# A one-core decoder layer: the first 1024 cross keys and values are made in the prologue, and the penalty rows are loaded ahead of the chunk's stores

## What is computed

```python
x = layernorm(x + self_attention(x))          # one key head and one value head shared by 16 query heads, no mask
x = layernorm(x + cross_attention(x, ctx))    # 6404 context keys, mask 1024 x 6404 (int32), 16 heads
x = layernorm(x + top1_experts(x))            # 8 experts, the best one times its softmax weight
```

## Time and profile before

| what | us |
|---|---|
| median of 3 runs | 467.17 (465.81 to 469.11) |
| profiled execution, its own time | 469.97 |
| its span in the profile | 467.7 |
| TensorE / VectorE / ScalarE / GpSimd busy | 440.9 / 396.7 / 358.4 / 245.1 |
| mean granted TensorE clock | 0.974 of full |

### The profile page before, as it was taken

The page is one execution under the profiler, slowest core; times in us unless marked ns, Lnnn a source line. Parts: engine busy times, 40 slices in busy tenths (PEclk is TensorE's granted clock), DMA queues, the critical chain, the costliest instruction groups (busy, mean ns, idle before and its releaser), DMA issues.

```text
span 467.7 us, 10803 instructions
## 1 busy us (share of the span) xinstructions
PE 440.9 (94%) x3885; PEld 176.7 (38%) x3887; DVE 396.7 (85%) x522; ACT 358.4 (77%) x704; POOL 245.1 (52%) x381
## 2 busy tenths in 40 slices
PE   8999999999899999799999999999999999999983
PEld 2433333333334443233343334333443443333441
DVE  4989999999699689689998999999999999941455
ACT  6328889688677877588968988889868788878723
POOL 4726879976799604122447644444447254320453
PEclk9889999999899999989999999999999999999978
DMA  5849968679680073211232346322212122110000
GB/s 129 322 115 315 283 218 297 264 263 332 228 329 13 3 135 80 65 45 46 84 90 69 101 93 111 92 60 58 88 51 70 39 81 69 47 29 26 5 22 25
DMA packets 24595, 56.07 MB, mean 120 GB/s; under 512 B 6442, under 2 KB 15928, under 8 KB 22492
## 3 DMA queue, kind: packets, MB, share of 16 engines
q0 software_dynamic: 7536, 37.91, 24.6%
q1 hardware_dynamic: 16424, 17.24, 14.1%
q10 hardware_dynamic: 580, 0.20, 0.2%
HBM read 45.60 MB, written 9.18 MB: 117 GB/s over the span
## 4 chain that ended last, share of the span: by engine, by line
PE 76%; DVE 10%; DMA 5%; issue 4%; ACT 2%; POOL 2%; POOLq 0%; DVEq 0%; ACTq 0%
PE O L1503 29%; PE ST L1739 15%; PE ST L1530 9%; PE RT L1732 7%; DVE mxs L935 6%; DMA Qs<-mxr 5%; PE RT L1518 4%; PE RT L1625 2%; PE ST L1632 2%; PE RT L1429 1%; PE O L1481 1%; ACT prob L1302 1%; PE RT L1587 1%; PE RT L1595 1%; DVE mxc L952 1%
## 5 line engine op out<-in xcount | busy, mean ns | idle before, releaser
L1302 ACT ACTIVATE prob<-ST 128x512 f32<-128x512 f32 x512 | 279.5, 599 | 59.0 <-PE ST L1530 29.3
L935 DVE TENSOR_REDUCE mxs<-RT 128x2 f32<-128x1024 f32 x128 | 153.0, 1222 | 14.6 <-PE RT L1518 13.5
L952 DVE TENSOR_REDUCE mxc<-RT 128x2 f32<-128x1024 f32 x128 | 152.8, 1221 | 5.8 <-PE RT L1732 5.4
L1739 PE MATMUL ST<-Qs,Kc 64*128 64x512 f32 x320 | 117.4, 450 | 0.0
L1732 PE MATMUL RT<-Kr,Qs 64*128 64x512 f32 (+1 forms) x384 | 114.4, 400 | 2.1 <-issue 2.1
L1503 PE MATMUL O<-prob,vst 128*9 128x256 f32 x1280 | 99.1, 381 | 1.7 <-ACT prob L1291 0.5
L1530 PE MATMUL ST<-Qs,Kself 64*128 64x512 f32 x256 | 96.7, 449 | 4.0 <-DMA Qs<-mxr 3.8
L1518 PE MATMUL RT<-Kself,Qs 64*128 64x512 f32 x256 | 89.3, 465 | 2.2 <-DVE Kself L912 0.9
L681 POOL DMA_DIRECT2D Kr<-kd x96 | 47.8, 502 | 75.9 <-PE RT L1732 60.8
L1503 PE MATMUL O<-prob,Vs 128*9 128x256 f32 x1024 | 81.0, 388 | 1.2 <-ACT osb L1246 0.3
L1739 PEld LDWEIGHTS ST<-Qs,Kc 64*128 64x128 f32 x320 | 50.5, 184 | 65.8 <-issue 38.7
(11 more groups left out here) (219 smaller groups left out, 327.4 us busy)
## 6 DMA issues: line engine op xcount, KB each, us to landing
big<-in_mask POOLq DMA_DIRECT2D x16, 1664.0 KB, 7.3
Kc<-kd POOLq DMA_DIRECT2D x64, 80.0 KB, 2.2
Kr<-kd POOLq DMA_DIRECT2D x64, 64.0 KB, 2.1
od_s<-osb SPq DMA_DIRECT2D x16, 128.0 KB, 2.5
kd<-Vx SPq DMA_DIRECT2D x4, 512.0 KB, 6.9
Qs<-qd_x SPq DMA_DIRECT2D x8, 256.0 KB
od_x<-osb SPq DMA_DIRECT2D x14, 128.0 KB, 1.7
Qs<-qd_s SPq DMA_DIRECT2D x12, 128.0 KB, 5.9
```

The lines of the kernel that those rows point to most:

```text
L935: freed(v.tensor_reduce(mxs[:, h % 2, c2, :].rearrange("p (f t) -> p f t", f=2)[:, :, q], bank[:, :].rearrange("p (f k) -> p f k", f=2), A ...
L952: return v.tensor_reduce(o[:, :, u % 4], src, AX.X, ALU.max)
L1302: freed(nc.scalar.activation(prob[:, s % SLOTS, f * HALF:(f + 1) * HALF], bank[:, :], ACT.Exp))
L1739: mm = mmul(o[:, :], Kc[STACK[f], b * P:(b + 1) * P], Qs[STACK[f], j, :], start=True, stop=not gen, skip_group_check=True)
```

## The change

* The loads of `wk_x`, `wv_x`, `bk_x` and the 1024 context rows `ctxn` (512 KB) move to the head of SyncE's queue, behind those of the self attention's small operands and ahead of `bo` and `x`.
* Beside rows 8 and 9 TensorE makes the keys (`first_keys`, one 512-column half each, into `ST[0]` and `ST[1]`), beside rows 11 and 13 the values (`first_values`, into `O` and `ST[0]`); row 10 keeps its `warm_up`, rows 12, 14 and 15 have nothing beside them.
* ScalarE evicts each half of the keys twice (rounded into `khi`, full into `kz`) and each half of the values once into a staging place `v_first`. GpSimd subtracts `khi` from `kz` behind its mask piece 0, and copies `v_first` into `Vx` at m = 13, ahead of the ones.
* The jobs at s = 42, 90 and 92 are gone with VectorE's and ScalarE's evictions there. The first self column waits for the new evictions.
* SyncE's turn h = 6 waits for GpSimd's subtraction, and the penalty rows are loaded in turn h = 13, ahead of the chunk's stores.

```diff
@@ RT_JOBS, ST_JOBS
-RT_JOBS = {42: ("k",), 76: ("s0 spread",), ...
+RT_JOBS = {76: ("s0 spread",), ...
-ST_JOBS = {66: ("bias",), 86: ("s0 turn",), 88: ("s0 q",), 90: ("v0",), 92: ("v1",), KV: ("vm",),
+ST_JOBS = {66: ("bias",), 86: ("s0 turn",), 88: ("s0 q",), KV: ("vm",),
+        v_first = vroom[:, 6 * HALF:8 * HALF]
@@ SyncE
             load(bv_s[:, :], row("bv_s").to_broadcast([P, DH]), "in_r")
+            for n_, b_ in (("wk_x", wk_x), ("wv_x", wv_x)):
+                load(b_[:, :], t[n_], "ctx_in")
+            load(bk_x[:, :], column("bk_x"), "ctx_in")
+            load(ctxn[:, :], t["ctxT"][:, KPAD - KS:KPAD], "ctx_in")
             load(bo["s"][:, :], row("bo_s").to_broadcast([P, D]), "in_bo")
...
-                if h == 4:
-                    load(ctxn[:, :], t["ctxT"][:, KPAD - KS:KPAD], "ctx_in")
                 if h in (6, 7, 8):
                     if h == 6:
-                        sp.wait_ge(S("rt_free"), number(RT_AT, "k"))
+                        sp.wait_ge(S("x_k_low"), 1)
...
                         load(pd[:, k * KC:(k + 1) * KC], penr[...], "pen_out")
-                if h == 14:
-                    more_keys()
                     sp.wait_ge(S("pen_out"), 16 * 5)
                     sp.wait_ge(S("k_clean"), 2)
                     for k_ in (Kr, Kc):
                         load(k_[PENROWS...], pd.to_broadcast([2, KUSE]), "pen_in")
+                if h == 14:
+                    more_keys()
@@ GpSimd
+                if m == 0:
+                    pool.wait_ge(S("x_k_full"), 2)
+                    g_.tensor_tensor(kz, kz, khi.bitcast(F32), ALU.subtract).then_inc(S("x_k_low"), 1)
                 if m in MAX_BETWEEN:
                     split_max(MAX_BETWEEN[m])
...
                 if m == 13:
                     pool.wait_ge(S("q_out"), 64)
+                    pool.wait_ge(S("x_v_copied"), 2)
+                    g_.tensor_copy(Vx[:, 0:SBLK, :, 0:DH], v_first.rearrange("p (b h d) -> p b h d", h=HEADS, d=DH)) \
+                        .then_inc(S("vx_first"), 1)
+                    pool.wait_ge(S("vx_first"), 1)
                     pool.wait_ge(S("kd_out"), 64)
@@ ScalarE
+            def first_keys(c):
+                w = slice(c * 512, c * 512 + 512)
+                act.wait_ge(S("x_k_ready"), c + 1)
+                act.wait_ge(S("ctx_in"), 64)
+                act.wait_ge(S("s_k_stack"), 2)
+                nc.scalar.activation(khi[:, w], ST[c][:, :], ACT.Identity, bias=bk_x[:, 0:1])
+                nc.scalar.activation(kz[:, w], ST[c][:, :], ACT.Identity, bias=bk_x[:, 0:1]).then_inc(S("x_k_full"), 1)
+            def first_values(k, bank):
+                act.wait_ge(S("x_v_ready"), k + 1)
+                act.wait_ge(S("q0_stack"), 2)
+                nc.scalar.copy(v_first[:, k * 512:(k + 1) * 512], bank[:, :]).then_inc(S("x_v_copied"), 1)
...
+            first_keys(0)
+            first_keys(1)
             max_copy(0, 2)
+            first_values(0, O)
+            first_values(1, ST[0])
@@ TensorE
                 if c == 0:
-                    pe.wait_ge(S("q_high"), 2)
-                    pe.wait_ge(S("q_full"), 2)
+                    pe.wait_ge(S("x_k_full"), 2)
+                    pe.wait_ge(S("x_v_copied"), 2)
...
+            def first_keys(c):
+                if c == 0:
+                    pe.wait_ge(S("ctx_in"), 64)
+                pe.wait_ge(S("q_high"), c + 1)
+                pe.wait_ge(S("q_full"), c + 1)
+                keys_into(ST[c], ctxn[:, c * 512:(c + 1) * 512], 512).then_inc(S("x_k_ready"), 1)
+            def first_values(k):
+                if k:
+                    pe.wait_ge(S("x_k_full"), 1)
+                values_into((O, ST[0])[k], ctxn, 4 * k, 4 * k + 4).then_inc(S("x_v_ready"), 1)
...
-                else:
+                elif r in (8, 9):
+                    first_keys(r - 8)
+                elif r in (11, 13):
+                    first_values((r - 11) // 2)
+                elif r == 10:
                     warm_up(O, 2)
```

More of the change, by code:

```diff
@@ L71, in place @@
     return (s - SELF) // NBLK, (s - SELF) % NBLK
-RT_JOBS = {42: ("k",), 76: ("s0 spread",), 79: ("s0 y",), 94: ("count",), 99: ("flags",), KV - 1: ("km",),
+RT_JOBS = {76: ("s0 spread",), 79: ("s0 y",), 94: ("count",), 99: ("flags",), KV - 1: ("km",),
            X(1, 3): ("s1 spread",), X(1, 5): ("s1 y",), X(9, 3): ("x0 spread",), X(9, 5): ("x0 y",),
@@ L261, in decoder_layer @@
             "mask_in0 mask_in1 mask_used mask_added mask_counts flags steered pen_made pen_out pen_in "
-            "ctx_in kd_out kd_more k_clean vx_ones kr0 kr1 kr2 kc0 kc1 vs0 vs1 mx_folded x_bias bias_tile dve_chain "
+            "ctx_in x_k_ready x_k_full x_k_low x_v_ready x_v_copied vx_first kd_out kd_more k_clean vx_ones kr0 kr1 kr2 kc0 kc1 vs0 vs1 mx_folded x_bias bias_tile dve_chain "
             "rt_ready rt_free st_ready st_free pv mx mx_part mx_split mx_turned mx_copied max_in0 max_in1 "
@@ L419, in _ @@
                 if h == 1:
-                    for n_, b_ in (("wq_x", wq_x), ("wk_x", wk_x), ("wv_x", wv_x)):
-                        load(b_[:, :], t[n_], "in_w")
+                    load(wq_x[:, :], t["wq_x"], "in_w")
                     for a, b_ in (("s", wo_s), ("x", wo_x)):
@@ L427, in _ @@
                     load(down[:, :], row("countdown").to_broadcast([P, NP]), "in_w")
-                    load(bk_x[:, :], column("bk_x"), "in_w")
                     load(bq["x"][:, :], column("bq_x"), "in_w")
@@ L633, in _ @@
                 if m == 7:
-                    pool.wait_ge(S("in_w"), 16 * 15)
+                    pool.wait_ge(S("in_w"), 16 * 12)
                     g_.tensor_copy(bv_wide[:, :], bv_x[:, :].to_broadcast([P, P])).then_inc(S("bias_tile"), 1)
@@ L799, in any_keys @@
                             cols_of(j + 1, None, pool.snap(n * (j + 1)))
-            pool.wait_ge(S("st_free"), number(ST_AT, "v1"))
+            pool.wait_ge(S("vx_ones"), 1)
             before = steps[0]
@@ L988, in cross_whole @@
                 whole_max(UNITS + U, mxc[:, U % 2, 0:2, :])
[L990 to L996, removed]
             def more_keys():
@@ L1135, in _ @@
                     dve.sem_inc(S("kd_more"), 1)
+                    dve.wait_ge(S("ctx_in"), 64)
                     more_keys()
@@ L1141, in _ @@
                 if s == 70:
-                    dve.wait_ge(S("in_w"), 16 * 15)
+                    dve.wait_ge(S("in_w"), 16 * 12)
                     mark(v.memset(downx[:, :], 0.0))
@@ L1153, in _ @@
                     residual("s", 0)
-                if s == 42:
-                    last_keys()
                 if s == 94:
@@ L1261, in x_queries @@
                 freed(nc.scalar.activation(xq_full[:, :], bank[:, :], ACT.Identity, bias=bq["x"][:, 0:1], scale=SCALE))
[L1263 to L1268, removed]
+            def first_keys(c):
[9 more added lines that the diff above has]
+                nc.scalar.copy(v_first[:, k * 512:(k + 1) * 512], bank[:, :]).then_inc(S("x_v_copied"), 1)
             def more_values():
                 bank = ST[ST_AT["vm"][2]]
+                act.wait_ge(S("vx_ones"), 1)
                 with act.Fori(0, n1) as i:
@@ L1342, in _ @@
                     x_queries(0)
-                if s in (90, 92):
-                    last_values((s - 90) // 2)
                 if s == KV:
@@ L1578, in bias_product @@
                 pe.wait_ge(S("bias_tile"), 1)
-                pe.wait_ge(S("in_w"), 16 * 15)
+                pe.wait_ge(S("in_w"), 16 * 12)
                 st_done(mmul(o[:, 0:D], bv_wide[:, :], wo_x[:, :], start=True, stop=True))
```

## The result

The changed kernel took 462.23 us (median of 4 runs, 460.7 to 465.59), the kernel before 468.11 us with the run beside it: ratio 0.9877, 95% interval 0.9839 to 0.9914. The forecast was 463.1 against 467.17, a ratio of 0.991, just inside the upper end of that interval: 4.1 us were forecast, 5.9 measured between the medians. The profiled execution of the changed kernel took 465.59 us, the longest of its four, with a span of 464.0 us, 3.7 us shorter than that of before.

A forecast was written before the change was run, and what follows sets the result against it. TensorE's chain through the self steps, 1.21 us each, was taken as the bound, VectorE right behind. -2.96 + 0.4 - 2.17 + 1.6 + 1.4 + 0.9 - 3.25 = -4.1 us from 467.17 gave 463.1 us, range 459.8 to 468.0.

The forecast's parts named there:

- the first cross row: From s = 112 to 114: penalty rows loaded earlier free TensorE's wait and the low clock behind it; -3.25 us.
- the values: At s = 90 and 92: eight value products leave TensorE's order, nothing takes their place; -2.17 us.
- the keys: Steps 42 to 45: key products and the wait for VectorE's evictions go from TensorE's order; -2.96 us.
- the prologue: Rows 8 to 15: added products run partly at low clock, first column late; +0.9 us, bounds -0.3 and +4.4.
- the clock behind the copy: After TensorE's longer gap at s = 75: one spell of low clock; +1.4 us, other bound 0.
- unit 8's gap: TensorE's 2.62 us wait for unit 8's maxima, held fixed; growing or going away (up to 4.1 us better) would refute.
- unit 6's maxima: Before s = 48: their load moves close to a mask piece and may land late; +0.4 us, bounds 0 and 1.2.
- Copy on GpSimd: At m = 13, ahead of the ones: its whole length delays TensorE's turn at s = 75; +1.6 us.
- rival B: No low clock at s = 75, or early clock return in the prologue, or both: about 461.1 us; chance 0.22.
- the first column: Sign at the prologue's end: between 31.2 and 33 us; after 34 the prediction is wrong.
- rival E: Mask pieces and key stores delay loads of maxima before units 6 and 7, 4.1 us each: 471.3 us; chance 0.10.
- the gap at s = 75: Sign: TensorE's wait for GpSimd there grows from 0.76 to about 2.4 us, with clock 0.50 behind it.

The follow-up runs named there:

- experiment 1: The kernel before with one edit: penalty rows loaded ahead of the chunk's stores, keys and values left at s = 42, 90 and 92; ratio 0.9878 to the kernel before.
- experiment 2: The changed kernel with the penalty rows put back behind the chunk's stores, so only keys and values move; ratio 0.9982 to the kernel before.
- experiment 3: The changed kernel with GpSimd's copy of the values into Vx at m = 1 instead of m = 13; ratio 0.9813 to the kernel before.
- experiment 4: The changed kernel with GpSimd's copy of the values made twice in a row at m = 13; ratio 0.9958 to the kernel before.
- experiment 5: The changed kernel with idle products of 512 columns added beside each of rows 4 to 7; ratio 0.9889 to the kernel before.
- experiment 6: The changed kernel with the idle bfloat16 pairs back beside rows 12, 14 and 15; ratio 0.9899 to the kernel before.
- experiment 7: The changed kernel with the keys' stores in SyncE's turns h = 3, 4, 5 instead of 6, 7, 8; ratio 0.9864 to the kernel before.

## Why the prediction was right, point by point

The number was right in part by luck. Three terms came as forecast and by their mechanism: the first cross row, the values and the keys. What the prologue and the clock behind the copy cost beyond their terms was paid back by unit 8's gap, which I had held fixed. I also gave 0.55 to "within 1% of before", and the median came out 1.2% below.

*The first cross row* (forecast -3.25): -3.49 in the changed kernel, -3.4 with that edit alone, and the gap back without it. Right, with the price. It rested on the issue of the load at 194.95 alone, as the trace named no releaser; experiments 1 and 2 show that this was enough.

*Values* (-2.17): -2.18. Right.

*Keys* (-2.96, +0.4 for unit 6's maxima): -2.94, and unit 6 had no wait at all. Right; the bound of 0 for the collision was the true one.

*Copy on GpSimd* (+1.6; bounds 1.0 and 2.1): 1.05, the size mis-chosen. I took the price of scattered single numbers; the runs of 8 cost what packed numbers do (1280 in 1.26 us). Its place was right, and experiments 3 and 4 show it with 0.77, 1.81 and 2.92 us. The other 0.6 us between turns 9 and 10 is the later landing of unit 9's maxima.

*The clock behind that gap* (+1.4, or 0): 2.6 in the profiled execution, since the spell lasted 7 us. It isn't sure, however: gaps of 1.80 to 1.82 us at this place were followed by the low level in the changed kernel and in experiment 5, and not in 6 and 7. That was rival B's condition, and it is one from execution to execution, not from kernel to kernel.

*The prologue* (+0.9; bounds -0.3 and +4.4): +2.69. This is the term that was mis-sized most. The mechanism was right, keys at half clock, but I let the clock return at the time of the trace of before. In nine profiled executions with the new prologue it returned between 25.6 and 26.9 us (five), at 28.1 (one) or at 29.9 (two), or never fell before 30 (one). Where it returned by 26.2 and the products beside the rows are the change's own (experiments 2, 3, 7) the first column came at 31.8 to 31.95 us, 0.3 to 0.5 later than before, with a return at 26.9 (experiment 4) at 32.29, and at 33.56 where it returned at 29.9. My 32.7 was for a single time of return; the term takes one of several values from execution to execution, and 0.9 is between them.

*Unit 8's gap* (held fixed): -1.91 in the profiled execution: 1.1 us less of wait, and no low spell after it, less 0.3 us of a new wait for GpSimd. I named it as what would make the prediction wrong. With E's collisions it is the same matter: the transfer engines are busy to 0.90 and more from 92 to 116 us (before 0.87 and more, but for one window at 0.63), and TensorE, 3 us ahead after s = 42, runs into that. In experiment 2 unit 8's wait is gone and turn 9 waits 2.81 us for GpSimd instead, which had waited for late mask pieces. So E came true in part, at turn 9 and at unit 4, but as a wait in the place of unit 8's and not on top of it.

So the sum of -4.1 held with terms that were off by up to 1.9 us each way: +1.8 in the prologue and +1.2 at the copy and its clock against -1.9 at unit 8, and the remaining stretches add up to -0.7. That they cancel is luck. Of the signs that I gave, the first column (33.56, not between 31.2 and 33), the gap at s = 75 (1.81, not about 2.4) and unit 8's gap (not fixed) missed. The part that decided the result was the last in the diff. Keys and values off TensorE's order are worth 5.1 us in their own steps, and by experiment 2 some 0.8 us of it were left, 2.4 at most by the interval: the copy, the prologue and the waits for maxima took the rest.

Three readings of mine were a little off and carry no term: in the trace of before the clock returned at 27.3 us, not 27.1; unit 8's wait is 2.62 us, not the 2.69 that rival E has; and unit 9's maxima took 2.4 us from their load's issue (125.02) to what waited for them (127.38), not 1.8.

What stays open: what sets the length of the low spells, in the prologue and near the end. The second takes part in every ratio here, by 0 to 3.3 us in the profiles; it is 1.5 us of experiment 1's 5.0, and whether the early copy has to do with it is not shown.

## What to carry to other kernels

Work taken off the bounding engine is worth its length only until the next engine's fixed order: before moving a job to another engine, look for the instruction there that the first engine already waits for, and place the job where the new engine idles long, and not in the loop that is waited for. A small load that gates a stage belongs ahead of every store on its queue that waits for something late; that edit gave here what the rest of the diff didn't. Where one job's removal moves the time little, compare the two traces at instructions that occur once per unit, and the gains and losses stand apart. Compare the stretches that no edit touches as well: here they differ by up to 3.3 us, almost as much as the best edit gained.

## What the runs showed of the hardware

* GpSimd copied 128 x 1024 float32 in runs of 8 with gaps of one in 1.05 us, but 128 x 832 single numbers at a distance of 9 in 1.66 to 1.73 us.
* After one and the same gap of TensorE (1.80 to 1.82 us before the turn at s = 75, four executions) the granted clock fell to 0.50 twice and stayed at 1.00 twice; after 0.77 it stayed, after 2.92 it fell, after 2.45 (experiment 5, turn 9) it stayed, and after 1.61 (experiment 6, unit 8) it fell. The length of the gap alone doesn't tell.
* After the same wait of 1.53 to 1.55 us near the end the granted clock was at 0.50 for 6.8 us in four of the eleven profiles, for 3.4 us in four, and never in three; the stretch behind turn 15 took 265.0 to 265.3, 263.5 to 263.6 and 261.9 us.
* The four runs of the changed kernel lie in the order of their mean granted clock: 465.59 us at 0.970, 462.81 and 461.65 at 0.977, 460.70 at 0.984. The 4.9 us between them are more than most terms of the sum, so one profiled execution can't price a term below some 2 us unless the same instructions are compared.
* 8 KB of maxima took 2.4 us from the issue of their load to what waited for them where the transfer engines were busy to 0.35 or less (before, 125.02 to 127.38 us), and 6.8 and 7.3 us beside a mask piece on GpSimd's queue, with busy shares of 0.77 and more for most of the time (changed kernel, units 4 and 8). The Trainium skill's page "DMA: Bandwidth & Descriptors", section "Queues, rings and completion order", has each transfer engine take turns between the queues; a small load still waits several microseconds here (58.72 to 65.52 us in the changed kernel, for unit 4).
